# Perceiver block with routed experts: order of the first loads and products, and of the small vector work between routing and experts

## The chip, the cores and the metric

One core of a Trainium2 chip runs the whole program in one launch. The metric is device time in microseconds (us), the median of the runs. The engines run their own instruction streams and meet at semaphores: TensorE (PE), VectorE (DVE), ScalarE (ACT), GpSimd (POOL) and SyncE (SP), which here only issues DMAs.

## The reference, cut to what matters

```python
x = x + xattn(ctx, ctx, layernorm(x))     # 64 batches, 32 queries, 257 keys, width 256
x = x + linear_attention(layernorm(x))    # 16 heads of 64, causal sums over 32 tokens, gate
x = x + experts(layernorm(x))             # 8 experts, hidden 1024, top 2 by softmax

# xattn
qp = q @ Wq.T + bq; kp = k @ Wk.T; vp = v @ Wv.T + bv
probs = softmax(qp @ kp.T / sqrt(256))
out = (probs @ vp) @ Wo.T + bo

# experts
scores = xt @ gate_w.T
top_vals, top_idx = top_k(scores, 2); top_w = softmax(top_vals)
h = silu(xt @ w1.T) * (xt @ w3.T)         # per expert
y = sum over the two picked experts of top_w * (h @ w2.T)
```

All data is float32. There are 2,048 tokens.

## The kernel before

Tokens are handled as NT = 16 tiles of 128 rows (four batches each). Every engine has its own list of steps, written out by hand; a semaphore for each product says how many tiles have it.

**Folded weights.** The cross-attention does not form keys and values. At the start PE forms m_qk from wq and wk (L544), c_qk from wk and bq (L549), the out-weight w_vo from wv and WoT (L556), and the bias from bv, WoT and bo (L561, L562). For the last, DVE spreads bv over 128 columns into bvb (L1259). ACT copies each result from PSUM (L954 to L960) and counts s_ev; PE waits for s_ev 6 before the first step, and POOL waits for the bias too. Before that PE waits for the loads l_wqk (wq, wk, bq), l_wx (wv, WoT, bv, bo) and l_con (the table of constants con, which also holds the identity for transposes).

**Cross-attention steps.** xstep(t) on PE: scores(t) L594, the transpose tr(t+2) of the normed rows L572, pv(t-1) L613 and L616, qk(t+1) L582, filler matmuls L642, the transposes of the probabilities p_tr(t) L604 and L605, c_tr(t-1) L626, proj(t-2) L635. FILL says how many filler matmuls a step gets; each filler appears as two instructions in the trace. On ACT a step is xT_ev(t+2), exp(t), qk_ev(t+1), pT_ev(t), cT_ev(t-1). On DVE it is maxes(t), last_row(t) (which makes p_last), norm(t-1), x1(t-2), ln(t+3), and in the first steps the statistics of the rows by quarter(q): quarter 0 ahead of all, quarter 1 in step -2, quarters 2 and 3 in step -1. In step 0 DVE also takes variance(0, FIRST_LN[1]) and ACT its square root; the table of functions on ACT is changed for this and back for exp.

**Loads.** SP issues the loads in this order: Wq, Wk, bq, rows quarter 0 (512 KB), con (395 KB), Wv, WoT, bv, bo (weights 256 KB each), ctxT(0) (1028 KB), row quarters 1 to 3; then in load(t) for each step a piece of the next stage's weights (256 KB, every second step), ctxT(t) (two buffers, freed by scores(t-2)), ctxN(t) (three buffers) and a small ctxL(t).

**From routing to experts.** After the linear attention (L536 to L538 products) come logits, and DVE picks the top two of the last four tiles in top_two(2) (max, then max_index for each tile). It adds up the counts (r_both), PE forms ranks (L817 to L819) and raises r_rank, and places() reads them. Filler matmuls (warm, L813, two instructions each) stand around ranks. DVE then marks the place of each picked token within a tile (in_slot) and the tile (in_tile); PE sums the row numbers into slots (L870) and raises r_rows. DVE writes slot_row (r_done), which the gather on POOL needs, and tile_e, the expert of each of the 39 slot tiles (r_map), which ACT waits for before its first w_hi. Of the two softmax weights, w_h is the float16 value and w_l what is left of it, scaled; weight_rows(h) multiplies both with in_tile into what_w, PE sums them (L877, r_tab), DVE forms slot_w.

**Experts.** Each float32 product is three products of rounded parts: high and low of the weights (w_hi by ACT L1139, w_lo by DVE L1570) and of the rows (xh by ACT, xl by DVE L1663). up(t) on PE takes four chunks of the weights of slot tile t (six matmuls each, L536 to L538) and waits for one low part at a time; it follows xtr(t) L888, the transpose of the gathered rows, and ahead of the first stands warm(5). DVE makes low parts 0 and 1 of the first tile with up_lo(0, range(2), expert(0)), then x_lo(0), then parts 2 and 3. expert(t) reads the expert's number from tile_e into a register.

## Time and profile before

| | us |
|---|---|
| median of 3 runs | 843.13 |
| lowest, highest | 838.98, 844.96 |
| profiled execution, its own time | 840.18 |
| its span, first to last instruction | 838.3 |
| PE busy | 798.5 (95%) |
| DVE busy | 640.2 (76%) |
| ACT busy | 565.7 (67%) |
| POOL busy | 282.0 (34%) |
| share of the chain that ended last | PE 88%, DVE 4%, issue 2% |
| mean granted PE clock | 0.982 |

The chain is followed back from the last instruction to what released each step. "issue" is time in which an engine waited for nothing that the profile shows. PE's busy time is modelled for pipelined matmuls. In rows of instructions the bracket gives the idle time of the engine before it and what ended it.

### The profile page before, as it was taken

The numbers are of one execution on the slowest core, as the hardware profiler recorded it, in microseconds if no ns is written. First come the engines' busy times: TensorE is split into PE (matmuls) and PEld (weight loads), VectorE is DVE, ScalarE is ACT, GpSimd is POOL, SyncE is SP. The second block draws the span as 40 slices with busy tenths as digits, with TensorE's granted clock in tenths as the row PEclk, the third lists the DMA queues.
The fourth block names the chain that finished last, engine by engine and source line by source line (L and its number), as shares of the span: only waits on it lengthen the run. The fifth ranks groups of instructions, "written<-read, shape, count | busy, mean of one in ns | idle before, by whom it ended". The sixth has DMA issues, their size and how long they took to land.

```text
span 838.3 us, 24109 instructions
## 1 busy us (share of the span) xinstructions
PE 798.5 (95%) x9278; PEld 696.6 (83%) x9278; DVE 640.2 (76%) x1033; ACT 565.7 (67%) x879; POOL 282.0 (34%) x190
## 2 busy tenths in 40 slices
PE   6999999999999999997897999999999999999993
PEld 5566588998999999996886888998889888898883
DVE  4445543756757575674788999999999999999992
ACT  2645456554656665472256899999899999988971
POOL 1333384020220202010001345555555555555541
PEclk9999999999999999999699999999999999999997
DMA  9999920000000000004962445544555445554452
GB/s 339 415 417 415 384 80 2 2 16 16 15 28 3 28 3 28 18 13 183 426 260 70 120 132 149 148 133 125 140 154 137 132 126 144 156 136 128 127 144 42
DMA packets 31771, 115.92 MB, mean 138 GB/s; under 512 B 4465, under 2 KB 11570, under 8 KB 26578
## 3 DMA queue, kind: packets, MB, share of 16 engines
q1 hardware_dynamic: 22834, 100.17, 33.4%
q0 software_dynamic: 8864, 14.69, 8.2%
q8 instruction: 57, 0.93, 0.4%
q14 instruction: 16, 0.13, 0.0%
HBM read 105.27 MB, written 9.57 MB: 137 GB/s over the span
## 4 chain that ended last, share of the span: by engine, by line
PE 88%; DVE 4%; issue 2%; ACT 1%; DMA 1%; SPq 0%; POOL 0%; POOLq 0%; DVEq 0%; ACTq 0%
PE ps L536 23%; PE ps L538 22%; PE ps L537 22%; PE ps L925 4%; PE ps L741 3%; PE ps L712 2%; PE ps L582 2%; PE ps L635 2%; PE ps L594 2%; PE ps L616 1%; PE ps L888 1%; PE ps L613 1%; PE ps L572 1%; PE ps L807 1%; DMA bor<-in_bo 1%
## 5 line engine op out<-in xcount | busy, mean ns | idle before, releaser
L1570 DVE TENSOR_TENSOR w_lo<-w,w_hi 128x1024 fp32r<-128x1024 f32 x156 | 187.4, 1224 | 1.1 <-issue 1.1
L522 POOL DMA_INDIRECT out_x<-y_sb,slot_row x39 | 123.7, 3173 | 117.9 <-ACT y_sb L1171 117.9
L1139 ACT ACTIVATE w_hi<-w 128x1024 fp32r x156 | 161.2, 1060 | 2.4 <-DVE tile_e L1614 2.4
L536 PE MATMUL ps<-w_hi,xh 128*128 128x512 f32 x312 | 125.8, 403 | 1.4 <-DVE xl L1663 1.3
L538 PE MATMUL ps<-w_hi,xl 128*128 128x512 f32 x312 | 122.0, 391 | 0.0
L537 PE MATMUL ps<-w_lo,xh 128*128 128x512 f32 x312 | 121.6, 390 | 0.0
L536 PE MATMUL ps<-xT_hi,wa_hi 128*128 128x256 f32 x384 | 109.4, 285 | 2.1 <-issue 1.0
L537 PE MATMUL ps<-xT_lo,wa_hi 128*128 128x256 f32 x384 | 107.9, 281 | 0.0
L538 PE MATMUL ps<-xT_hi,wa_lo 128*128 128x256 f32 x384 | 107.8, 281 | 0.0
L1150 ACT ACTIVATE w_hi<-w_sb 128x1024 fp32r<-128x1024 f32 x78 | 82.6, 1063 | 27.7 <-DMA w_sb<-in_w 15.2
L510 POOL DMA_INDIRECT xs_sb<-xn_d,slot_row x39 | 67.3, 1726 | 98.8 <-PE ps L888 78.4
L536 PE MATMUL ps<-w_hi,hh 128*128 128x256 f32 x312 | 91.9, 295 | 2.9 <-DVE hl L1670 2.9
L1649 DVE TENSOR_TENSOR w_lo<-w_sb,w_hi 128x1024 fp32r<-128x1024 f32 x78 | 92.1, 1225 | 2.1 <-ACT w_hi L1150 2.1
L538 PE MATMUL ps<-w_hi,hl 128*128 128x256 f32 x312 | 88.9, 285 | 0.0
L537 PE MATMUL ps<-w_lo,hh 128*128 128x256 f32 x312 | 88.7, 284 | 0.0
L536 PEld LDWEIGHTS ps<-xT_hi,wa_hi 128*128 128x128 f32 x384 | 72.3, 188 | 3.4 <-issue 2.4
L537 PEld LDWEIGHTS ps<-xT_lo,wa_hi 128*128 128x128 f32 x384 | 72.4, 188 | 0.4
L538 PEld LDWEIGHTS ps<-xT_hi,wa_lo 128*128 128x128 f32 x384 | 72.3, 188 | 0.0
L1029 ACT ACTIVATE neg<-ps 128x512 f32<-128x512 f32 x64 | 38.3, 598 | 47.5 <-PE ps L538 47.5
L536 PEld LDWEIGHTS ps<-w_hi,xh 128*128 128x128 f32 x312 | 58.5, 188 | 13.5 <-DVE xl L1663 2.0
L538 PEld LDWEIGHTS ps<-w_hi,xl 128*128 128x128 f32 x312 | 58.5, 188 | 12.8
L537 PEld LDWEIGHTS ps<-w_lo,xh 128*128 128x128 f32 x312 | 58.6, 188 | 11.1
(219 smaller groups left out, 1767.3 us busy)
## 6 DMA issues: line engine op xcount, KB each, us to landing
w_sb<-in_w SPq DMA_DIRECT2D x78, 512.0 KB, 4.5
ctx_t<-in_ctxT SPq DMA_DIRECT2D x16, 1028.0 KB, 9.0
ctx_n<-in_ctxN SPq DMA_DIRECT2D x16, 1024.0 KB
w<-in_w SPq DMA_DIRECT2D x8, 2048.0 KB, 14.8
stage<-in_w_a SPq DMA_DIRECT2D x16, 256.0 KB, 8.7
x_all<-in_x SPq DMA_DIRECT2D x4, 512.0 KB, 9.3
out_x<-x_all POOLq DMA_DIRECT2D x8, 256.0 KB, 3.2
xn_d<-xn_first POOLq DMA_DIRECT2D x6, 256.0 KB, 2.8
```

The lines of the kernel that those rows point to most:

```text
L510: pool.indirect_dma_start(xs_sb[:, :], None, xn_d, bass.IndirectOffsetOnAxis(slot_row[:, t:t + 1], 0)).then_inc(f_xs, 16)
L522: pool.indirect_dma_start(out, bass.IndirectOffsetOnAxis(slot_row[:, t:t + 1], 0), y_sb[:, :], None, compute_op=ALU.add).then_inc(f_st, 16)
L536: pe.matmul(dst, l_hi, r_hi, start=first, stop=False)
L537: pe.matmul(dst, l_hi, r_lo, start=False, stop=False)
L538: return pe.matmul(dst, l_lo, r_hi, start=False, stop=last)
L741: m = pe.matmul(ps[h * HD:(h + 1) * HD, 4 + b, (s * FC + c) * T:(s * FC + c + 1) * T], v_sb[rows, s, (2 * c + h) * HD:(2 * c + h + 1) * HD ...
L925: m = pe.transpose(ps[:, 4 + c // 4, (c % 4) * P:(c % 4 + 1) * P], h_sb[:, c * P:(c + 1) * P], ident)
L1029: act.activation(neg[:, n % 2, :], ps[:, n % 4, :], ACT.Relu, scale=-1.0).then_inc(a_neg, 1)
L1139: act.activation(w_hi[:, c, :].rearrange("p (c n) -> p c n", c=DC), w13[:, bass.ds(e, 1), c % 2, :, c // 2 * 512:(c // 2 + 1) * 512].rearr ...
L1150: act.activation(w_hi[:, 4 + c, :], src, ACT.Copy).then_inc(f_dhi, 1)
L1570: dve.tensor_tensor(w_lo[:, c, :].rearrange("p (c n) -> p c n", c=DC), w13[:, bass.ds(e, 1), c % 2, :, c // 2 * 512:(c // 2 + 1) * 512].re ...
L1649: dve.tensor_tensor(w_lo[:, 4 + c, :], src, w_hi[:, 4 + c, :].bitcast(F32), ALU.subtract).then_inc(f_dlo, 1)
```

## The change

Four edits:

1. SP loads row quarter 0 first; Wq and Wk follow; bq gets its own semaphore l_bq and goes behind con; ctxT(0) goes ahead of Wv, WoT, bv and bo.
2. On PE the products for c_qk move into step -2 (key_bias), behind tr(0). Those for w_vo and the bias move into step 0 (out_weight, out_bias), between qk(1) and p_tr(0), in banks 6 and 7; c_tr(0) and proj(0) get waits for their evictions. ACT's evictions move likewise: c_qk in step -2, w_vo and bias behind qk_ev(1) in step 0. DVE makes bvb in step -1, ahead of quarters 2 and 3. Filler matmuls stay in step -1 only (before: one in -2, two in -1, two in 0, one in 1).
3. On DVE the difference of the two top logits (dv) is taken inside top_two(2), between max and max_index. The steps from e1p to w_h move from behind slot_row to ahead of places(). tile_e moves behind slot_row.
4. The expert's number e0 is read once, ahead of the wait for r_tab, and only low part 0 is made ahead of x_lo(0); parts 1 to 3 follow it.

```diff
@@ -302,7 +302,7 @@
-    l_con, l_wqk, l_wx, l_wo, l_z = (sem(n) for n in ("l_con", "l_wqk", "l_wx", "l_wo", "l_z"))
+    l_con, l_wqk, l_bq, l_wx, l_wo, l_z = (sem(n) for n in ("l_con", "l_wqk", "l_bq", "l_wx", "l_wo", "l_z"))
     XQ = 4
@@ -357,16 +357,16 @@
+        load_x(0)
         weight(wq, "Wq", l_wqk)
         weight(wk, "Wk", l_wqk)
-        sp.dma_start(bqc[:, :], a["bq"]).then_inc(l_wqk, 16)
-        load_x(0)
         sp.dma_start(con[:, :], a["con"]).then_inc(l_con, 16)
+        sp.dma_start(bqc[:, :], a["bq"]).then_inc(l_bq, 16)
+        load_ctxT(0, 0)
         weight(wv, "Wv", l_wx)
...
             sp.dma_start(buf[:, :], a[name]).then_inc(l_wx, 16)
-        load_ctxT(0, 0)
         for q in range(1, XQ):
@@ -538,29 +538,36 @@
-        pe.wait_ge(l_wqk, 16 * 3)
+        pe.wait_ge(l_wqk, 16 * 2)
         for dc in range(DC):
...
         m.then_inc(s_mm, 1)
-        for dc in range(DC):
+        pe.wait_ge(l_con, 16)
+
+        def key_bias():
+            pe.wait_ge(l_bq, 16)
+            for dc in range(DC):
+                for ec in range(DC):
+                    m = pe.matmul(ps[:, 1, dc:dc + 1], wk[:, ec, dc * P:(dc + 1) * P], bqc[:, ec:ec + 1],
+                                  start=ec == 0, stop=ec == DC - 1)
+            m.then_inc(s_mm, 1)
+            pe.wait_ge(s_ev, 2)
+
+        def out_weight():
+            pe.wait_ge(l_wx, 16 * 4)
+            for dc in range(DC):
+                for ec in range(DC):
+                    m = pe.matmul(ps[:, 6, dc * D:(dc + 1) * D], wv[:, ec, dc * P:(dc + 1) * P], wo[:, ec, :],
+                                  start=ec == 0, stop=ec == DC - 1)
+            m.then_inc(s_mm, 1)
+
+        def out_bias():
+            pe.wait_ge(s_bvb, DC)
             for ec in range(DC):
-                m = pe.matmul(ps[:, 1, dc:dc + 1], wk[:, ec, dc * P:(dc + 1) * P], bqc[:, ec:ec + 1],
-                              start=ec == 0, stop=ec == DC - 1)
-        m.then_inc(s_mm, 1)
-        pe.wait_ge(l_wx, 16 * 4)
-        pe.wait_ge(l_con, 16)
-        for dc in range(DC):
-            for ec in range(DC):
-                m = pe.matmul(ps[:, 2, dc * D:(dc + 1) * D], wv[:, ec, dc * P:(dc + 1) * P], wo[:, ec, :],
-                              start=ec == 0, stop=ec == DC - 1)
-        m.then_inc(s_mm, 1)
-        pe.wait_ge(s_bvb, DC)
-        for ec in range(DC):
-            pe.matmul(ps[:, 3, 0:D], bvb[:, ec, :], wo[:, ec, :], start=ec == 0, stop=False)
-        pe.matmul(ps[:, 3, 0:D], ones[0:1, :], bor[0:1, :], start=False, stop=True).then_inc(s_mm, 1)
-        pe.wait_ge(s_ev, 6)
+                pe.matmul(ps[:, 7, 0:D], bvb[:, ec, :], wo[:, ec, :], start=ec == 0, stop=False)
+            pe.matmul(ps[:, 7, 0:D], ones[0:1, :], bor[0:1, :], start=False, stop=True).then_inc(s_mm, 1)
@@ -622,6 +629,8 @@
             wait(pe, x_cT, t)
+            if t == 0:
+                pe.wait_ge(s_ev, 3)
             for dc in range(DC):
@@ -631,11 +640,13 @@
             wait(pe, x_x1, t)
+            if t == 0:
+                pe.wait_ge(s_ev, 6)
             for dc in range(DC):
...
-        FILL = {-2: 1, -1: 2, 0: 2, 1: 1}
+        FILL = {-1: 2}
@@ -645,8 +656,13 @@
             pv(t - 1, 1 - p)
+            if t == -2:
+                key_bias()
             qk(t + 1, 1 - p)
             fill(t)
+            if t == 0:
+                out_weight()
+                out_bias()
             p_tr(t, p)
@@ -952,12 +968,16 @@
         act.activation(m_qk[:, :, :], ps[:, 0, :].rearrange("p (c d) -> p c d", c=DC), ACT.Copy).then_inc(s_ev, 1)
-        act.wait_ge(s_mm, 2)
-        act.activation(c_qk[:, :], ps[:, 1, 0:DC], ACT.Copy).then_inc(s_ev, 1)
-        act.wait_ge(s_mm, 3)
-        act.activation(w_vo[:, :, :], ps[:, 2, :].rearrange("p (c d) -> p c d", c=DC), ACT.Copy).then_inc(s_ev, 1)
-        act.wait_ge(s_mm, 4)
-        act.activation(bias[:, :], ps[:, 3, 0:D], ACT.Copy).then_inc(s_ev, 3)
+
+        def key_bias_ev():
+            act.wait_ge(s_mm, 2)
+            act.activation(c_qk[:, :], ps[:, 1, 0:DC], ACT.Copy).then_inc(s_ev, 1)
+
+        def out_ev():
+            act.wait_ge(s_mm, 3)
+            act.activation(w_vo[:, :, :], ps[:, 6, :].rearrange("p (c d) -> p c d", c=DC), ACT.Copy).then_inc(s_ev, 1)
+            act.wait_ge(s_mm, 4)
+            act.activation(bias[:, :], ps[:, 7, 0:D], ACT.Copy).then_inc(s_ev, 3)
@@ -1000,10 +1020,14 @@
             xT_ev(t + 2, p)
+            if t == -2:
+                key_bias_ev()
             exp(t, p)
...
             qk_ev(t + 1, 1 - p)
+            if t == 0:
+                out_ev()
             pT_ev(t, p)
@@ -1254,9 +1278,11 @@
         dve.wait_ge(l_con, 16)
-        dve.wait_ge(l_wx, 16 * 4)
-        for ec in range(DC):
-            dve.tensor_scalar(bvb[:, ec, :], ones, bvc[:, ec:ec + 1], None, ALU.mult).then_inc(s_bvb, 1)
+
+        def value_bias():
+            dve.wait_ge(l_wx, 16 * 4)
+            for ec in range(DC):
+                dve.tensor_scalar(bvb[:, ec, :], ones, bvc[:, ec:ec + 1], None, ALU.mult).then_inc(s_bvb, 1)
@@ -1322,6 +1348,7 @@
             if isinstance(t, int) and t == -1:
+                value_bias()
                 quarter(2)
@@ -1476,6 +1503,8 @@
             wait(dve, g_max, ts.stop)
+            if ts.stop == NT:
+                dve.tensor_tensor(dv[:, :], m8[:, :, 1], m8[:, :, 0], ALU.subtract).then_inc(r_d, 1)
             for t in range(ts.start, ts.stop):
@@ -1579,7 +1608,12 @@
         dve.tensor_tensor(scan[0][:, 7 + NT, :], scan[0][:, 6 + NT, :], both[:, NT - 1, :], ALU.add).then_inc(r_both, 1)
-        dve.tensor_tensor(dv[:, :], m8[:, :, 1], m8[:, :, 0], ALU.subtract).then_inc(r_d, 1)
+        dve.wait_ge(r_e1, 1)
+        link(dve.tensor_scalar(e1p[:, :], e1[:, :], 1.0, None, ALU.add))
+        link(dve.reciprocal(top_w[:, :, 0], e1p[:, :]))
+        link(dve.tensor_tensor(top_w[:, :, 1], e1[:, :], top_w[:, :, 0], ALU.mult))
+        flat = top_w[:, :, :].rearrange("p t k -> p (t k)")
+        link(dve.tensor_copy(w_h[:, :], flat))
         places()
@@ -1608,36 +1642,32 @@
         in_slots(range(ACT_Q, TOP * NT // 4))
-        link(dve.tensor_tensor(cmp2[:, :, :], con[:, C_TILE:C_TILE + SLOT_TILES].rearrange("p (t a) -> p t a", a=1).to_broadcast([P, SLOT_TILES, E]),
-                               end[:, 4:].rearrange("p (a e) -> p a e", a=1).to_broadcast([P, SLOT_TILES, E]), ALU.is_ge))
-        link(dve.reduce_sum(tef[:, :], cmp2[:, :, :], AX.X))
-        dve.tensor_scalar(tile_e[:, :], tef[:, :], float(E - 1), None, ALU.min).then_inc(r_map, 1)
         def weight_rows(h):
...
+        link(dve.tensor_tensor(cmp2[:, :, :], con[:, C_TILE:C_TILE + SLOT_TILES].rearrange("p (t a) -> p t a", a=1).to_broadcast([P, SLOT_TILES, E]),
+                               end[:, 4:].rearrange("p (a e) -> p a e", a=1).to_broadcast([P, SLOT_TILES, E]), ALU.is_ge))
+        link(dve.reduce_sum(tef[:, :], cmp2[:, :, :], AX.X))
         dve.wait_ge(r_rows, 1)
...
         dve.scalar_tensor_tensor(slot_row[:, :], ps[:, 6, 0:SLOT_TILES], -1.0, spare[:, :], ALU.add, ALU.add).then_inc(r_done, 1)
-        dve.wait_ge(r_e1, 1)
-        link(dve.tensor_scalar(e1p[:, :], e1[:, :], 1.0, None, ALU.add))
-        link(dve.reciprocal(top_w[:, :, 0], e1p[:, :]))
-        link(dve.tensor_tensor(top_w[:, :, 1], e1[:, :], top_w[:, :, 0], ALU.mult))
-        flat = top_w[:, :, :].rearrange("p t k -> p (t k)")
-        link(dve.tensor_copy(w_h[:, :], flat))
+        dve.tensor_scalar(tile_e[:, :], tef[:, :], float(E - 1), None, ALU.min).then_inc(r_map, 1)
         link(dve.tensor_tensor(w_d[:, :], flat, w_h[:, :], ALU.subtract))
...
         weight_rows(1)
+        dve.wait_ge(r_map, 1)
+        e0 = expert(0)
         dve.wait_ge(r_tab, 1)
...
         dve.wait_ge(r_done, 1)
-        up_lo(0, range(2), expert(0))
+        up_lo(0, range(1), e0)
@@ -1682,7 +1712,7 @@
         x_lo(0)
-        up_lo(0, range(2, 4), expert(0))
+        up_lo(0, range(1, 4), e0)
         for t in range(2):
```

## Rows read from the trace of the kernel before

**Rows 1.** Chain of the first 60 us: start us, us, what
```profile
18.42 1.02 PE ps L594 x16
...
20.25 1.28 ACT L983
...
45.37 1.08 PE ps L594 x16
```

**Rows 2.** Busy us by stage: PE, PEld, DVE, ACT, POOL; PEclk, DMA share, GB/s
```profile
21.00:23.00 2.00, 0.87 (x6) 0.42 (x4) 0.86 (x4) 1.61 (x5) 1.92 (x3) 1.00 1.00 414
...
35.00:46.00 11.00, 10.97 (x110) 6.86 (x106) 4.79 (x17) 4.65 (x16) 3.29 (x4) 1.00 1.02 415
```

**Rows 3.** DMA view, 0 to 10 us, 40 slices of 0.25 us
```profile
GB/s 0 0 0 0 0 0 0 98 90 213 381 356 225 303 426 419 294 214 98 131 230 295 246 295 307 341 301 379 290 366 305 349 353 328 398 334 423 448 403 345
```

**Rows 4.** Timeline of SP: issue of ctxT(5), start us, us
```profile
35.35 0.33 SPq L358 DMA_DIRECT2D ctx_t<-in_ctxT  x1
```

**Rows 5.** DMA view of 35.3 to 35.5 us: size, us to landing
```profile
ctx_t<-in_ctxT SPq DMA_DIRECT2D x1, 1028.0 KB, 10.0
```

**Rows 6.** Timeline, 0 to 24 us: start us, us, engine line, out<-in [idle before]
```profile
5.58 3.78 PE L544 MATMUL ps<-wk,wq 128*128 128x256 f32 x8 [5.58 <-DMA bqc<-in_bq]
...
11.23 1.99 PE L556 MATMUL ps<-wo,wv 128*128 128x256 f32 x8 [0.88 <-DMA bor<-in_bo]
...
11.61 0.48 DVE L1259 TENSOR_SCALAR bvb<-con,bvc 128x128 f32<-128x128 f32 x2
...
13.06 1.03 PE L561 MATMUL ps<-wo,bvb 128*128 128x256 f32 x4
...
14.92 1.40 DVE L1214 BATCH_NORM_STATS2 bn<-x_all 128x6 f32<-128x256 f32 x4 [2.18 <-DMA x_all<-in_x]
...
16.76 2.70 DVE L1214 BATCH_NORM_STATS2 bn<-x_all 128x6 f32<-128x256 f32 x8
...
22.70 0.44 PE L604 MATMUL ps<-con,prob 128*128 128x128 f32 x2 [1.13 <-DVE p_last L1290]
...
23.18 0.59 PEld L594 LDWEIGHTS ps<-ctx_t,qkT 128*32 128x32 f32 x16 [0.22 <-DMA ctx_t<-in_ctxT]
```

**Rows 7.** Timeline, 431 to 453 us, columns as in rows 6
```profile
431.06 0.61 DVE L1494 TENSOR_TENSOR prod<-chosen,ps 128x128 f32<-128x128 f32 x2 [0.83 <-PE ps L819]
...
442.50 0.17 DVE L1625 TENSOR_SCALAR e1p<-e 128x16 f32<-128x16 f32 x1
...
443.13 3.90 ACT L1139 ACTIVATE w_hi<-w 128x1024 fp32r x4 [2.43 <-DVE tile_e L1614]
...
443.41 0.19 DVE L1630 TENSOR_TENSOR w_d<-top_w,w_h 128x32 f32<-128x32 f32 x1
...
443.86 0.83 DVE L1618 TENSOR_TENSOR what_w<-in_tile,w_h 128x640 f16<-128x640 f32 x1
...
446.95 1.25 PE L877 MATMUL ps<-what_w,in_slot 128*128 128x80 f16 x16 [0.72 <-DVE what_w L1619]
...
448.45 3.08 PE L813 MATMUL ps<-con 128*128 128x256 f32 x10
...
449.73 2.36 DVE L1570 TENSOR_TENSOR w_lo<-w,w_hi 128x1024 fp32r<-128x1024 f32 x2 [1.06 <-issue]
452.01 0.42 DVE L1663 TENSOR_TENSOR xl<-ps,xh 128x256 fp32r<-128x256 f32 x1
...
452.48 0.50 PE L536 MATMUL ps<-w_hi,xh 128*128 128x512 f32 x1 [0.94 <-DVE xl L1663]
```

**Rows 8.** DMA view of 443.2 to 444 us: first gather, us to landing
```profile
xs_sb<-xn_d,slot_row POOLq DMA_INDIRECT x1, 2.9
```

**Rows 9.** Busy time by stage, columns as in rows 2
```profile
402.00:404.00 2.00, 0.74 (x5) 0.65 (x5) 1.97 (x6) 0.38 (x1) 0.00 (x0) 0.55 1.03 426
...
447.00:448.00 1.00, 1.00 (x17) 1.00 (x17) 0.00 (x0) 0.02 (x1) 0.00 (x0) 0.50 0.00 0
...
490.00:510.00 20.00, 20.00 (x123) 17.71 (x122) 20.00 (x22) 18.20 (x24) 9.68 (x5) 1.00 0.47 131
```

## Prediction

> **What bounds the kernel now.** I read the views from the whole to the part: the page's shares and chain (the table above), then the chain of the first 60 us [rows 1], the busy table by stage [rows 2], the DMA queue and its landings [rows 3 to 5], and last the instructions in order of time in the two stretches that the change touches [rows 6, 7]. TensorE (PE) carries 88% of the chain. The change touches no stage in which PE works through long products; it touches the start (0 to 30 us) and the passage between routing and experts (430 to 453 us), where the chain leaves PE.
>
> In the cross-attention after the start there are two bounds side by side. PE is busy 10.97 of 11 us, and the DMA engines are busy all the time at 415 GB/s [rows 2]. One step takes half of 11.06 us and needs one ctxT (1028 KB), one ctxN (1024 KB) and half a piece of 256 KB: 2.24 MB, which at 415 GB/s takes 5.4 us. PE's step is 5.5 us, so the DMA wins only about 0.1 us a step. At the start it has no lead at all: the scores of step 1 wait for ctxT(1) at 23.18 [rows 6], and ctxT(5), issued at 35.35 [rows 4], lands 10.0 us later [rows 5], at 45.35, just when its scores begin (45.37 in the chain) [rows 1]. The reader should see here that no earlier start of PE brings step 1 or step 5 forward, unless the bytes come earlier.
>
> Between routing and experts VectorE (DVE) is the bound: it makes the weight rows from 443.86, PE sums them at 446.95, DVE then reads an expert's number (1.06 us "issue"), makes two low parts, and only then xl, for which the first expert product waits until 452.48 [rows 7].
>
> **The start.** What each part does, in time of before's trace:
>
> - The products of wq and wk (L544, 3.78 us) begin at 5.58 [rows 6]. Now the 512 KB of the first rows go ahead of the two weights and bq behind; at the 300 to 350 GB/s of that stretch [rows 3] this is about +1.5 us less bq's wait: begin 6.5, end 10.3. The first rows land before these weights, but their normalisation still waits for con, whose bytes stand behind the same ones as before (about 9.3).
> - Out of PE's queue ahead of the first step go the out-weight products (1.99 us, L556), their bias products (1.03 us for four, and two more of that width, 0.5) and the wait for bo at 11.23 [rows 6]. With transposes, key bias (under the 1.99 us of L556, since it is as many but narrower matmuls), qk(0) and two filler matmuls between, I get scores(0) at 14.7 instead of 18.42 [rows 1]: 3.7 us earlier.
> - That gain meets DVE. Before maxes(0) it must take the statistics of x quarters 1 to 3, and quarter 1 lands at 14.92. The bytes ahead of it are the same set in another order, so this doesn't move by the reordering. From there: 1.40 us, one xn, and from 16.76 on 2.70 us for two quarters, to 19.46 [rows 6]. Now bvb (0.48 us for two) stands in this queue as well, so maxes(0) would start 0.4 later than in before. What is won instead: ACT loads its exp table (1.28 us at 20.25 [rows 1]) while it waits, and not behind the maxes. So exp(0) begins near 20.5 instead of 21.54, 1.0 earlier. Its p_last, on which p_tr(0) (22.70) waited, comes 1.0 earlier too [rows 6].
> - The moved products now sit on PE between qk(1), which ends at about 18.2 (xn(2) at 16.65 leads), and p_tr(0): 3.5 us, to 21.7, about when p_last is there. Their two evictions (1.0 us) stand on ACT ahead of pT(0). They eat some of the 1.0. I get p_tr(0) at 21.7, tr(3) 0.4 us earlier than before.
> - scores(1) then waits for ctxT(1), whose time is set by bytes. The filler of step 1 (two matmul instructions, 0.5 us by the eight of L556) falls away, but behind it p_tr(1) needs p_last: I take 0.2 us. Together PE would be some 0.4 us ahead at step 2 and is caught by the DMA again by step 5.
>
> What can still come is an earlier DMA stream. Before, the moved rate falls to 98 and 131 GB/s between 4.5 and 5.0 us [rows 3], behind bq's small packets with the x load not yet begun. With 512 KB as the first transfer the queue doesn't run dry: at 320 GB/s lost for some 0.5 us at two thirds, and some at the neighbours, 0.4 us. The bounds are 0 (bq's and bv's small packets only move within the stream) and 0.9 (the dip and its neighbours gone). **Term 1: -0.4 us (0 to -0.9)**, carried by PE to the end of the stage and on.
>
> A page and a row differ on the stream. The row shows 415 GB/s from HBM to SBUF over 11 us [rows 2]. The Trainium skill, DMA: Bandwidth & Descriptors, section Where 436 GB/s comes from, says that for such transfers the HBM side binds at about 358 GB/s. By that figure a step would last 6.2 us and PE would wait in every one; the trace does not agree, and I keep the row.
>
> **Routing.** dv moves between max and max_index, into the chain of part 2: about +0.1 (an estimate, half of the 0.18 of its neighbours' form [rows 7], since small independent ones overlap). The four small instructions from e1p (442.50) to w_h, before w_d at 443.41, take 0.91 us and go into the wait for the ranks [rows 7]. That wait is 0.83 us, and dv's place in it falls free (0.1): next to nothing is left over. Should this cover be gone, they cost up to 0.9 there and the gain below is nil. **Term 2: +0.1.**
>
> **Weight rows.** w_d starts 0.91 earlier, less the reordering of tile_e behind slot_row, which leaves the sum of DVE's work the same: what_w starts at 443.0 instead of 443.86, and PE's last half of them (1.25 us at 446.95) begins at 446.1 [rows 7]. tile_e comes 0.4 us later, and with it ACT's four w_hi (443.13, 3.90 us): they end at 447.4, and the next that needs ACT is xh, after the transpose on PE near 447.8. So it is hidden; xh would be late only from a delay of about 0.8. Behind tile_e's wait nothing else of ACT stands. The gather of the first rows goes out behind slot_row, which is done when e1p starts at 442.50 and now comes 0.1 earlier; a us later on GpSimd's side and 2.9 us from issue to landing [rows 8] make some 446.4, ahead of need.
>
> **Low parts.** The expert's number is read before the wait for r_tab, under PE's 1.25 us: of the 1.06 us "issue" ahead of w_lo [rows 7] some 0.9 go. So w_lo(0) starts at 448.0 instead of 449.73 and ends at 449.2, and xl (0.42) follows it instead of the second one (1.2 less): 449.65, against 452.43 in before, 2.8 earlier. The other three low parts follow at 1.2 us each (2.36 for two [rows 7]), so the second is ready 1.2 us after the first product can begin.
>
> But PE has ten filler matmuls in its queue ahead of the first expert product: 3.08 us at the halved clock [rows 7, 9]. They follow the transpose, 0.85 earlier than now, and end at about 450.65. In before they had 0.94 us to spare; now they are what ends last. The first product starts at 450.65 instead of 452.48. From there DVE and PE are both full (20.00 of 20.00 us each from 490 on [rows 9]), and the first times and low parts of tile 1 depend on these products by the same distances, so the shift stays. **Term 3: -1.85**, bounds 0 (something not seen takes the place of xl) and -2.8 (full clock, no filler in the way).
>
> **Sum:** -0.4 + 0.1 - 1.85 = -2.15 us. The profiled execution took 840.18 us (838.3 span and 1.9 around it) and would take 838.0. It lies 2.95 under the median of the three runs (843.13); I put the change on the median: 841.0.
>
> **Rivals.**
> 1. *The clock stays up in the passage.* It is halved at 447 [rows 9], where PE had waited 1.84 and 0.72 us for weight rows [rows 7]; now the first wait is 0.9 shorter. Without the fall L877 takes 0.75, the filler 2.4: first product at 449.7, and the end at -3.0: 840.1. For it: shorter waits. Against: a second wait and its place remain.
> 2. *The intended gain arrives whole.* scores(0) is 3.7 earlier and all follows: -3.7 + 0.1 - 1.85 = -5.45, 837.7. Against it stand quarter 1 at 14.92 and ctxT(1) at 23.18 [rows 6].
> 3. *The passage brings nothing:* the small work spills over its 0.83 us and the filler, or ACT's later w_hi, holds xl: only term 1 and 2, and at most half of term 3: -1.2, 841.9 (to 842.8 for none).
> 4. *Slower.* Filler is taken from the first steps and PE has gaps before 17 and after 22 us. From 402 to 404 PE was busy 0.74 of 2 us and the clock went to 0.55 [rows 9]. If it falls so at 17 to 23, the 3.5 us of moved products take 7, p_tr(0) comes at 25.2 instead of 22.70, the DMA is then ahead and hides nothing: +2.5 there, term 1 hidden, +0.1 and -1.85: +0.75, 843.9. It decides once the products end after 22.7. Against: from 21 to 23 PE was busy 0.87 of 2 us and the clock stayed 1.00 [rows 2]. The Trainium skill, TensorE: Matmul & The Clock Gate, section HAM oscillation, says that long enough idle gaps on PE halve its clock; by that rule filler is not to be taken away, and the two rows disagree on whether gaps of this size do it.
>
> **Chances.** Forecast 0.45; rival 1 0.18, rival 2 0.07, rival 3 0.17, rival 4 0.13. The centres of 1, 3 and 4 lie within 840.1 and 843.9. The three runs before spread by 6 us around their median, which is more than the change, so I add some 3 us below and 1 us above: 836.5 to 845.0. A measurement of this kernel can tell about 1% (8.4 us) from no change; none of the cases reaches that. Faster by over 1%: 0.04 (rival 2 with a low draw), slower by over 1%: 0.03, within 1%: 0.93.
>
> **What would show it.** In the profile after: scores(0) near 14.7; 8 statistics ending near 19.5 with maxes right behind; exp(0) within 0.1 us of nmx and no table load between; out-weight products ending before p_last; a wait for ctxT at step 1 and near step 5, at 22.7 and 45.0; first what_w near 443.0 less the shift of the start; w_lo(0) within 0.4 us of slot_w; the first expert product right behind the filler and 1.9 us (beside the start's shift) earlier. I am wrong if ctxT(5) lands over 1 us earlier or later than 45.0, if clock in the first 25 us shows under 1.00, if xl is still what the first product waits for, or if some wait among tiles 1 to 5 of the experts gives the 1.85 us back.

## The result and the profile after

| | before | after |
|---|---|---|
| median, us | 844.05 (12 runs) | 836.00 (12 runs) |
| lowest, highest | 838.98, 846.63 | 831.99, 837.58 |
| profiled execution, its own time | 840.18 | 833.98 |
| its span | 838.3 | 832.1 |
| PE busy | 798.5 | 796.2 |
| mean granted PE clock | 0.982 | 0.981 |

The ratio is 0.9909, 95% interval [0.989, 0.9928]: 7.7 us faster. That is just inside the 1% that the prediction called its limit of what can be told, but outside its range (836.5 to 845.0) by 0.5 us, and more than three times its 2.15 us. The sign was right. The forecast was put on a median of before of 843.13 from three runs; over twelve it is 844.05.

The first view of the kernel after is the timeline of the start (start us, us, engine line, out<-in, in brackets the idle time before). The rows answer [rows 6].

```profile
7.02 3.78 PE L544 MATMUL ps<-wk,wq 128*128 128x256 f32 x8 [7.02 <-DMA wk<-in_Wk]
...
14.70 1.08 PE L601 MATMUL ps<-ctx_t,qkT 128*32 128x257 f32 x16
...
16.88 1.89 PE L562 MATMUL ps<-wo,wv 128*128 128x256 f32 x8
...
20.19 0.44 PE L611 MATMUL ps<-con,prob 128*128 128x128 f32 x2
...
21.93 1.07 PE L601 MATMUL ps<-ctx_t,qkT 128*32 128x257 f32 x16 [1.20 <-DMA ctx_t<-in_ctxT]
```

The same stretch on DVE and ACT:

```profile
13.69 1.41 DVE L1238 BATCH_NORM_STATS2 bn<-x_all 128x6 f32<-128x256 f32 x4 [4.55 <-DMA x_all<-in_x]
...
15.71 2.71 DVE L1238 BATCH_NORM_STATS2 bn<-x_all 128x6 f32<-128x256 f32 x8
18.34 0.41 DVE L1307 TENSOR_REDUCE mx<-ps 128x1 f32<-128x257 f32 x1
...
16.58 1.28 ACT L1003 ACT_TABLE_LOAD   x1
18.97 0.48 ACT L1003 ACTIVATE prob<-ps,nmx 128x257 f32<-128x257 f32 x1 [1.10 <-DVE nmx L1309]
```

Scores(0) run at 14.70, quarter 1 lands at 13.69, the table load lies in ACT's wait, and PE then waits for ctxT(1) until 21.93.

The passage from routing to experts, which answers [rows 7]:

```profile
428.55 0.61 DVE L1523 TENSOR_TENSOR prod<-chosen,ps 128x128 f32<-128x128 f32 x2 [1.67 <-PE ps L835]
...
440.43 0.82 DVE L1648 TENSOR_TENSOR what_w<-in_tile,w_h 128x640 f16<-128x640 f32 x1
...
442.05 0.75 PE L893 MATMUL ps<-what_w,in_slot 128*128 128x80 f16 x16 [0.92 <-DVE what_w L1649]
...
443.52 0.75 PE L893 MATMUL ps<-what_w,in_slot 128*128 128x80 f16 x16 [0.72 <-DVE what_w L1649]
...
444.35 2.32 PE L829 MATMUL ps<-con 128*128 128x256 f32 x10
...
444.88 1.23 DVE L1599 TENSOR_TENSOR w_lo<-w,w_hi 128x1024 fp32r<-128x1024 f32 x1
...
446.03 0.42 DVE L1693 TENSOR_TENSOR xl<-ps,xh 128x256 fp32r<-128x256 f32 x1
...
446.50 0.50 PE L536 MATMUL ps<-w_hi,xh 128*128 128x512 f32 x1
```

From prod (the picks multiplied with their ranks) to the first expert product it takes 17.95 us; before it took 21.42 (431.06 to 452.48 in [rows 7]). The weight sums take 0.75 us, not 1.25, and the filler 2.32, not 3.08.

A third part of the gain lies where nothing was changed. In the linear attention DVE starts each tile with an instruction att<-att,den. Laid over each other by it, the profiled executions differ by -1.1 us at 150 and -1.0 at 264, by -0.5 at 295, -1.7 at 332 and -4.57 at 398 to 402. The timeline of PE shows what went. Of before:

```profile
319.63 0.39 PE L536 MATMUL ps<-xT_hi,wa_hi 128*128 128x256 f32 x1 [1.03 <-issue]
...
379.45 1.28 PE L712 MATMUL ps<-qT,kT 64*32 64x32 f32 x128 [0.25 <-issue]
383.19 0.39 PE L536 MATMUL ps<-wa_hi,xT_hi 128*128 128x512 f32 x1 [2.46 <-issue]
```

And of after at the same place of the program:

```profile
377.56 1.33 PE L728 MATMUL ps<-qT,kT 64*32 64x32 f32 x128
378.82 0.50 PE L536 MATMUL ps<-wa_hi,xT_hi 128*128 128x512 f32 x1
```

Before, PE stood 2.46 us behind 128 short products and 1.03 us at 319.63, each time for nothing that the profile shows ("issue"; I call such an idle time a stall). After, neither is there. Others are: 0.69 us at 281.57, where before has none over 0.3, and 1.83 at 402.31, where before has 0.76 at 405.77. From 60 to 440 us the stalls of over 0.3 us add up to 6.30 us before and 4.12 after.

The whole pair: start -1.1, the two stalls and their surroundings -3.5, last tile to the end of top_two +0.5 (the longer stall at 402.31 lies here), ranks +1.5 (they stand behind filler at the low clock: prod came 3.92 us after the picks, before 2.38), passage -3.5, experts -0.2. The sum, from unrounded terms, is -6.2.

### The profile page after: what moved, and what is told of

The parts are those of the page before. It is cut to its first block, busy times and chain, and to the rows that moved or that the text cites. A ratio compares the mean times of both kernels' runs of the same rounds, so it can differ in the third digit from the quotient of the medians.

```text
span 832.1 us, 24093 instructions
## 1 busy us (share of the span) xinstructions
PE 796.2 (96%) x9270; PEld 695.7 (84%) x9270; DVE 637.9 (77%) x1033; ACT 564.5 (68%) x879; POOL 281.5 (34%) x190
## 4 chain that ended last, share of the span: by engine, by line
PE 89%; DVE 4%; DMA 3%; issue 2%; ACT 1%; POOL 0%; POOLq 0%; SPq 0%; DVEq 0%; ACTq 0%
PE ps L536 23%; PE ps L538 22%; PE ps L537 22%; PE ps L941 4%; PE ps L757 3%; PE ps L728 2%; PE ps L589 2%; PE ps L646 2%; PE ps L601 2%; PE ps L623 1%; DMA ctx_t<-in_ctxT 1%; PE ps L904 1%; PE ps L620 1%; PE ps L829 1%; PE ps L823 1%
## 6 DMA issues: line engine op xcount, KB each, us to landing
w<-in_w SPq DMA_DIRECT2D x8, 2048.0 KB, 14.3
```

## The experiments

The kernels of the table ran 6 to 12 times each, and before 23 to 33 times beside them on the same chip; the ratios are to those runs. Each run has one profiled execution, to which all places and stalls below belong. All compute the whole reference.

| run | median, us | ratio to before [95%] |
|---|---|---|
| start_only | 838.18 | 0.9932 [0.9912, 0.9952] |
| passage_only | 840.18 | 0.9951 [0.9928, 0.9975] |
| fill_only | 841.32 | 0.9975 [0.9951, 0.9999] |
| small_only | 842.22 | 0.9978 [0.9947, 1.0008] |
| lo_only | 842.12 | 0.9986 [0.9959, 1.0013] |
| products_only | 846.01 | 1.0039 [1.0006, 1.0072] |
| loads_only | 847.25 | 1.0032 [1.0005, 1.006] |
| after_pad4 | 837.93 | 0.9949 [0.9921, 0.9976] |
| after_pad4_late | 838.61 | 0.9946 [0.9917, 0.9975] |
| after_warm1 | 836.54 | 0.9911 [0.9871, 0.9951] |
| after_nofill | 834.46 | 0.9902 [0.9874, 0.993] |

One execution each: before_again 844.34, after_pad2_late 833.36, after_pad8_late 842.29, after_pad16_late 857.47.

### Start and passage apart

**start_only**: edits 1 and 2. **passage_only**: edits 3 and 4. The diffs are the parts of the change above.

```diff
 start_only:   edits 1, 2 as in the change; passage as before
 passage_only: edits 3, 4 as in the change; start as before
```

> Edits 1 and 2 alone (loads, first products, filler). Theory A: the loads bring the stream of bytes about 1.1 us earlier, and PE's idle stretches named issue at 319.6 (1.03), 383.2 (2.46) and 389.6 us (1.36) go or shrink because PE's instruction stream is shorter ahead of them and its fetched blocks begin elsewhere: about -4.5 us in all, and the same places and sizes of issue stretches before 400 us as in the changed kernel. Rival B: these stretches fall anew in every execution, whatever the code: -1.1 us in the median, and other stretches than in the changed kernel.

> Edits 3 and 4 alone. PE's stream ahead of the routing is as before. Theory A: the issue stretch of 2.46 us before 383.2 stays; the passage from the ranks to the first expert product is 2 to 3.5 us shorter; time -2.5 to -3.5 us. Rival B: the same time, but the stretch of 2.46 us is likely gone or elsewhere.

Measured: -5.7 us and -4.1 us by the ratios (intervals 4.1 to 7.4 and 2.1 to 6.1). The passage took 20.91 us in start_only and 17.93 in passage_only. start_only has the stalls of the changed kernel (0.98 at 385.83), passage_only those of before (1.28 at 322.48, 2.17 at 385.73), as theory A had it in both. So the start's edits brought at least as much as the passage, where the prediction gave them 0.4. The two together make -9.8, more than the 7.7 of the whole change; their intervals are wide enough for this.

**before_again**, unchanged:

> The kernel before, profiled once more. Theory A: the same issue stretches on PE before 400 us at the same distance from the start, 0.69, 1.03, 2.46 and 1.36 us within 0.3. Rival B: other places or sizes.

Stalls of 1.13 us at 320.29 and 2.17 at 383.45 were there again: they belong to the kernel, not to one execution. The passage took 21.15; in fill_only, loads_only and products_only, where it is unchanged too, 21.40 or 21.41.

### Filler or stream length

```diff
-        FILL = {-2: 1, -1: 2, 0: 2, 1: 1}
+        FILL = {-1: 2}
```

> Only the filler matmuls of steps -2, 0 and 1 are taken out (four fewer, eight instructions in the trace), nothing else. The start itself can win 0.2 us at most. Theory A: the issue stretches before 400 us lie and measure otherwise than before and the time changes by 1 to 3.5 us. Rival B: no change of the time (within 0.5 us).

It gained 2.1 us (interval 0.1 to 4.1). The start of its profiled execution was one of the slowest (scores(0) at 20.92), but its PE timeline has no stall at 320 or 383. With four fewer filler matmuls, PE's stream is 16 instructions of the trace shorter there.

To tell the filler from the length, **after_pad4** restores the length by four products that nothing reads:

```diff
             proj(t - 2, p)
+            if t == 0:
+                for _ in range(4):
+                    pe.matmul(ps[:, 1, 0:1], ident, con[:, 0:1], start=True, stop=True)
```

> The changed kernel with four matmuls of one column added on PE ahead of the scores of step 1, where PE waits 1.2 us for ctxT(1). They have no use and lengthen PE's stream by the same number of instructions (16 in the trace) that the taken filler had. Theory A (the stalls hang on where PE's stream falls into its blocks): the issue stretches of before come back near 320 (1.1 us) and 383 (2.2 us), and the time is 3 us longer than the changed kernel's (some 839 against 836). Rival B: the stretches stay as in the changed kernel and the time with them (836).

The start was as in the changed kernel (scores(1) at 22.33, the first att<-att,den at 149.94 against 149.64), and both stalls came back. PE of after_pad4:

```profile
319.11 0.28 PE L538 MATMUL ps<-xT_hi,wa_lo 128*128 128x256 f32 x1 [0.86 <-issue]
...
382.39 0.50 PE L536 MATMUL ps<-wa_hi,xT_hi 128*128 128x512 f32 x1 [2.17 <-issue]
```

The median rose by 1.9 us, against the 3 expected; the intervals of the two ratios overlap a little (up to 0.9928 and from 0.9921), so this difference alone is not certain. **after_pad4_late** puts the same four into step 12, far from the start:

```diff
-            if t == 0:
+            if t == 12:
```

> The changed kernel with the same four one-column products as in the run after_pad4, but put in step 12 (near 90 us) instead of step 0, so that nothing of the start is touched. Theory A (the stalls of PE near 319 and 382 depend on how many instructions stand in PE's stream ahead of them): the stalls come back (0.8 us or more near 320, 2 us or more near 383), the first att<-att,den still stands near 149.8, and the median is 837.5 to 839, 1.5 to 3 us above the changed kernel. Theory B (the stalls follow from something in the first steps, such as the start's timing or its loads): no stall above 0.5 us there and the time of the changed kernel, 836.

```profile
321.04 0.28 PE L538 MATMUL ps<-xT_hi,wa_lo 128*128 128x256 f32 x1 [0.84 <-issue]
...
384.77 0.80 PE L536 MATMUL ps<-wa_hi,xT_hi 128*128 128x512 f32 x1 [2.71 <-issue]
```

Theory A held: both are back, and the median is 2.6 us over the changed kernel's, of which the padding itself takes about 0.9 in step 12, where it is not hidden by a DMA (the first att<-att,den came at 151.20, not at the 149.8 expected).

Then three lengths more, one execution each: two, eight and sixteen of the padding products in step 12.

```diff
-                for _ in range(4):
+                for _ in range(2):      # 8, 16
```

> The changed kernel with two of the one-column products in step 12 (eight more trace instructions, half way between the changed kernel's stream and that of before). Theory A (a stall shows only where the end of a block of PE's instructions falls on a stretch of short ones, so each placement has its own set): sum of the issue stalls from 190 to 400 us between the 2.8 us of the changed kernel and the 6 us of before, with one of the two near 320 and 383 there. Theory B (the stalls of 320 and 383 are there or not by chance from execution to execution): no relation to the length; either both or none.

> The same with eight products (32 more trace instructions, 16 beyond the length of before). Theory A: the stalls near 320 and 383 are there as in before, or have moved by a few instructions; those near 198 and 283 may be gone or longer. Theory B: they are absent as often as present.

> The same with sixteen products (64 more trace instructions). Theory A: the set of stalls changes again; if blocks are short against 64 instructions it returns to one of the sets already seen, if they are long the stalls of 320 and 383 move to other lines of the same stage. Theory B: no relation.

PE of after_pad2_late, then of after_pad8_late:

```profile
380.92 0.50 PE L537 MATMUL ps<-wa_lo,xT_hi 128*128 128x512 f32 x1 [1.07 <-issue]
...
386.23 0.29 PE L731 MATMUL ps<-qT,kT 64*32 64x32 f32 x15 [1.05 <-issue]
```

```profile
320.64 0.26 PE L731 MATMUL ps<-qT,kT 64*32 64x32 f32 x5 [0.78 <-issue]
380.15 0.24 PE L760 MATMUL ps<-att,v_sb 32*64 32x32 f32 x2 [1.02 <-issue]
385.42 0.27 PE L731 MATMUL ps<-qT,kT 64*32 64x32 f32 x8 [2.21 <-issue]
```

The sum of PE's stalls of over 0.3 us, by the number of PE's matmuls in the page:

| matmuls | kernels | 315 to 395 us | 60 to 440 us |
|---|---|---|---|
| 9266 | after_nofill | 1.83 | 4.35 |
| 9270 | after, start_only, fill_only, and after_warm1 (5 fillers fewer, all behind this stretch) | 0.97 to 1.25 | 4.12 to 4.67 |
| 9274 | after_pad2_late | 2.46 | 4.17 |
| 9278 | before, before_again, small_only, lo_only, passage_only, products_only, loads_only, after_pad4, after_pad4_late | 3.46 to 4.85 | 5.77 to 8.07 |
| 9286 | after_pad8_late | 4.01 | 8.05 |
| 9302 | after_pad16_late | 3.29 | 13.31 |

Sixteen products moved them again: 1.34 us at 186.87, 1.32 at 369.43, 2.26 at 397.95, 4.55 at 427.45 are the longest. after_pad2_late has 3.1 us of stalls from 190 to 400, between the changed kernel's 2.3 and before's 5.5, as theory A had it. The nine executions of 9278 matmuls, from eight kernels, all have the two stalls at the same two places of the program, and the four of 9270 have neither. Theory B of these three runs, chance from execution to execution, is out. Over the whole stretch the nine have 6.63 us of stalls on the mean and the six shorter ones 4.27: 2.4 us less, close to what fill_only gained (2.1) and the two pads of four gave back (1.9 and 2.6).

The place is fixed more closely than by the length. Count PE's matmuls from the front (the x in PE's busy column, from 0 to just ahead of a stall). Of before, of after_pad4, then of before and of after:

```profile
0.00:383.18 383.18, 366.97 (x6276) 1.00 0.32 121
0.00:382.38 382.38, 366.03 (x6276) 1.00 0.32 122
0.00:405.76 405.76, 384.79 (x6654) 1.00 0.34 132
0.00:402.30 402.30, 383.51 (x6654) 0.99 0.35 134
```

In the 17 traces the stalls between 190 and 415 us stand behind 2464, 4242 or 4243, 5004 or 5005, 6276, 6403 or 6654 matmuls (not each one in every execution); with eight and sixteen products in step 12 there are further ones, each about a whole multiple of 127 matmuls away from one of these. So the stall stays at its place in the stream, and the program is shifted under it. On the DMA side, the queue for instructions moves blocks of 16,384 bytes. Its packets of the 2.46 us stall (before, 380.0 to 383.3 us):

```profile
q8 instruction: 1, 0.02, 2.4%
```

This packet ended at 381.82, 1.37 us ahead of the stall's end. The distance is 1.2 to 1.6 us for every stall of over 0.3 us from 60 to 440 us in the 17 traces, with one exception (1.72, at the 4.55 us stall). PE goes on a nearly fixed time after a block has come in. All this fits PE waiting for its own instructions; no run varied the blocks themselves.

The longest stall also has a consequence that the pair of before and after doesn't show. Eleven executions have the stall of 2.2 to 2.7 us behind 6276 matmuls; in eight of them (small_only, lo_only, passage_only, products_only, loads_only, after_pad4_late, after_pad8_late, after_pad16_late) the granted clock fell to its lower level within 1.2 us of the stall's end, for 3.4 to 10.2 us. In the six executions without it the clock did not fall there. From the matmul behind the stall to the 522nd after it, stalls left out, PE took 31.4 to 33.3 us where the clock fell and 29.3 to 30.7 where not. How often it falls in the executions that were not profiled is not known; before, before_again and after_pad4 had the stall without the fall.

after_pad16_late also shows something else. It was 24 us slower than after_pad2_late, 12.6 of them by the first att<-att,den. Its busy table by stage (PE, PEld, DVE, ACT, POOL, PEclk, DMA share, GB/s):

```profile
32.00:35.00 3.00, 1.45 (x19) 0.53 (x17) 1.43 (x3) 0.56 (x3) 2.87 (x4) 1.00 1.01 412
35.00:37.00 2.00, 2.00 (x16) 0.89 (x16) 0.87 (x4) 0.88 (x3) 0.00 (x0) 0.69 1.03 427
37.00:40.00 3.00, 3.00 (x20) 2.02 (x13) 0.48 (x1) 0.00 (x0) 0.00 (x0) 0.50 1.01 410
```

PE had waited 1.55 us for a ctxT (scores(2) at 34.06), then the clock fell to its lower level and the next step took 8.74 us (scores at 34.06 and 42.80) instead of 5.53, before any padding had run. Step 12 with its padding followed (3.8 us for the sixteen), and scores(13) at 97.62 took 1.94 us, at half speed again. The fall near 35 is the mechanism of rival 4, in one of nine executions with the new start, behind a DMA wait.

### The start taken apart

**products_only** moves only the products (edit 2 without the new FILL), **loads_only** only the loads (edit 1).

```diff
 products_only:
-        load_x(0)
         weight(wq, "Wq", l_wqk)
         weight(wk, "Wk", l_wqk)
+        sp.dma_start(bqc[:, :], a["bq"]).then_inc(l_bq, 16)
+        load_x(0)
         sp.dma_start(con[:, :], a["con"]).then_inc(l_con, 16)
...
-        FILL = {-1: 2}
+        FILL = {-2: 1, -1: 2, 0: 2, 1: 1}
```

(against the changed kernel's start; ctxT(0) behind bo again.)

> Of the start, only the new place of the products of edit 2 (key bias, out weight, bias, and DVE's bvb), with the old order of loads and the old filler; PE's stream is as long as before. Theory A (the moved products bring the start's gain, as they stand where PE waits anyway and their slow executions are hidden): first att<-att,den near 150, scores(0) at 16 to 17, ratio 0.995 to 0.998; the stalls near 320 and 383 are there, as the stream has its old length. Theory B (the loads bring it): att<-att,den between 150 and 155 as in before and ratio 0.998 to 1.001.

> Before with only the new order of the first loads and bq's own semaphore; all products, filler and the passage as before. Theory A (loads bring nothing by themselves, since the out-weight products still stand ahead of the first scores): ratio 0.999 to 1.002, the out-weight products later than in before (WoT lands behind ctxT(0)), scores(0) 19 to 22, and scores(1) 24 or later. Theory B (the earlier DMA stream carries the gain): scores(1) at 22.3 or earlier, ratio 0.994 to 0.997.

Both are slower than before, by 3.3 and 2.7 us (intervals 0.5 to 6.1 and 0.4 to 5.1). Theory A of products_only missed (first att<-att,den at 153.21); of loads_only, theory A named the right places (scores(1) at 24.29) but a ratio of at most 1.002. PE of products_only:

```profile
17.83 1.08 PE L601 MATMUL ps<-ctx_t,qkT 128*32 128x257 f32 x16
...
20.88 1.89 PE L562 MATMUL ps<-wo,wv 128*128 128x256 f32 x8
...
24.18 0.44 PE L611 MATMUL ps<-con,prob 128*128 128x128 f32 x2
```

The scores start only at 17.83, so the moved products end at 24.18, where before p_tr(0) stood at 22.70 [rows 6]. In loads_only the out-weight products wait for bo behind ctxT(0), until 12.55, and the scores come at 19.68:

```profile
12.55 1.99 PE L557 MATMUL ps<-wo,wv 128*128 128x256 f32 x8 [0.97 <-DMA bor<-in_bo]
...
19.68 1.08 PE L595 MATMUL ps<-ctx_t,qkT 128*32 128x257 f32 x16
```

Together, and with four fewer fillers, they gain 5.7 us (start_only), of which the stalls are some 2: the products have to be gone from ahead of the scores, and the scores' data have to be early. Both together with the old fillers were not run.

What the start brought can be read from the first att<-att,den. With the old start it stood at 150.74 (before), 149.97, 152.66, 155.26 and 154.00 in five executions (mean 152.5), and at 154.45 in fill_only; with the new one at 149.64 (after), 150.04, 149.94, 149.78 and 149.62 (mean 149.8; after_nofill and the runs with four or more products in step 12 left aside). The profiled execution of before was one of its good ones: the gain is 2.7 us on the mean and 1.1 in that pair. PE of small_only:

```profile
11.41 3.78 PE L556 MATMUL ps<-wo,wv 128*128 128x256 f32 x8 [1.06 <-DMA bor<-in_bo]
...
21.17 1.08 PE L594 MATMUL ps<-ctx_t,qkT 128*32 128x257 f32 x16
```

So in the four late executions PE, and not the bytes, was what scores(1) waited for: ctxT(1) had landed at 22.0 to 23.3 and the scores came at 24.4 to 25.8. With the new start the out-weight products stand where PE waits for ctxT(1) anyway, behind the rise, and took 1.89. In the two executions of that start with a late rise and the filler of step -1 (16.2 in start_only, 15.9 in after_pad2_late) scores(1) came at 22.76 and 22.30, and the first att<-att,den at 150.04 and 149.62, as in those with a rise at 11.2 to 12.4. The new start makes the kernel indifferent to when the clock rises, within that reach.

**after_nofill** takes the last filler out as well:

```diff
-        FILL = {-1: 2}
+        FILL = {}
```

> The changed kernel without the last filler of the first steps (eight more trace instructions less in PE's stream). Theory A (where the stream falls decides the stalls near 320 and 383, and a further shift can bring them back, move them or leave them out): the stalls stand at another place than in the changed kernel or are the same as in it; time within 2 us of the changed kernel, with the difference equal to the sum of the stalls. Theory B (filler in step -1 keeps the clock up): granted clock under 1.00 in the first 25 us and the first att<-att,den over 1 us later than 149.6, ratio to before 0.993 or more.

```profile
16.54 1.94 PE L601 MATMUL ps<-ctx_t,qkT 128*32 128x257 f32 x16 [0.81 <-ACT qkT L995]
```

Here scores(0) took 1.94 us instead of 1.08 and the first att<-att,den came at 152.04, 2.4 later than in the changed kernel. The first rise of the clock came at 19.6, later than in any other execution. That this is for want of the filler is not shown: up to 13.7 us both kernels run the same stream, and in six of the eight executions with the new start and the filler the clock had risen by 12.4, before the filler began. And the time is the changed kernel's (0.9902 against 0.9909, intervals overlapping), so theory B missed in the ratio, and theory A held, with the stalls behind the same counts of matmuls as elsewhere. The 2.4 shrink to 1.7 at the first expert product and 0.5 at the end; why is open.

### The passage taken apart

**small_only** is edit 3 alone, **lo_only** edit 4 alone.

```diff
 small_only:
-        dve.tensor_tensor(dv[:, :], m8[:, :, 1], m8[:, :, 0], ALU.subtract).then_inc(r_d, 1)
+        dve.wait_ge(r_e1, 1)
+        link(dve.tensor_scalar(e1p[:, :], e1[:, :], 1.0, None, ALU.add))
...
 lo_only:
+        dve.wait_ge(r_map, 1)
+        e0 = expert(0)
         dve.wait_ge(r_tab, 1)
...
-        up_lo(0, range(2), expert(0))
+        up_lo(0, range(1), e0)
```

> Of the change only edit 3 (dv, the steps e1p to w_h and tile_e moved). Theory: what_w starts 0.9 us earlier after the ranks, the waits of PE for it are shorter (0.92 instead of 1.84 us) and the clock stays at 1.00 until the first expert product: -0.9 and -0.5 for the second L877 group, up to the first product -1.4 us. Rival (the shorter wait has no bearing on the clock): it falls near 447 to 454 us as in the four profiles without the edit, -0.9 us.

> Of the change only edit 4 (the expert's number read ahead of r_tab, one low part ahead of xl). DVE could have xl 2.0 us earlier. Theory: the clock falls here as in before, and the filler of 3.08 us holds PE, so the first product comes only some 0.9 us earlier than before after the ranks and starts right behind the filler. Rival: the filler does not hold it, -2.0 us.

From prod to first expert product took 19.98 and 20.04 us, each 1.4 less than in before and the three others with 21.4; both together 17.93 to 17.95, 3.5 less. Neither alone is told from no change by its ratio. The missing 0.7 us is the filler at the low clock: in lo_only xl was ready at 456.14 and the first product began at 456.88. PE of lo_only, then of small_only:

```profile
451.24 0.75 PE L877 MATMUL ps<-what_w,in_slot 128*128 128x80 f16 x16 [1.83 <-DVE what_w L1619]
452.71 1.25 PE L877 MATMUL ps<-what_w,in_slot 128*128 128x80 f16 x16 [0.72 <-DVE what_w L1619]
...
456.88 0.58 PE L536 MATMUL ps<-w_hi,xh 128*128 128x512 f32 x1
```

```profile
452.68 0.75 PE L877 MATMUL ps<-what_w,in_slot 128*128 128x80 f16 x16 [0.72 <-DVE what_w L1622]
...
457.70 0.50 PE L536 MATMUL ps<-w_hi,xh 128*128 128x512 f32 x1 [1.88 <-DVE xl L1664]
```

In lo_only PE had waited 1.83 us, the clock fell, and although xl was early the first product stood behind the slow filler, at 456.88, just as the forecast had it for the whole change. With edit 3 the wait is 0.92 us and the clock stays at its upper level. Of the 17 executions, seven had the wait of 1.83 us (before, before_again, start_only, fill_only, lo_only, loads_only, products_only) and in all seven the clock fell behind it, in start_only only 1 us behind the first product. Nine had 0.91 or 0.92 us (all with edit 3 but after_warm1) and in none it fell, not even in small_only, where PE waited a further 1.88 us for xl. The edits and the wait go together here, so this says nothing of other places.

**after_warm1** takes filler away ahead of ranks, since the ranks stood behind it at the low clock:

```diff
-            warm(6)
+            warm(1)
```

> The changed kernel with one filler matmul instead of six ahead of the ranks. DVE has the counts ready while PE still has filler in its queue (5.3 us at the halved clock); without it the ranks follow the counts. If that queue is what costs: -1 to -1.5 us (834.7). Rival: with less filler the clock is low for longer and what follows takes more: 0 or up to +2 us.

prod came 3.07 us after the picks instead of 3.92, but the passage behind took 19.12 us instead of 17.95 (the low clock that had begun at 417.8 lasted to 434.9, where after's ended at 428.1), and the time is the changed kernel's. No gain, as the rival had it.

## Why the prediction was wrong, point by point

**The start, term 1 (-0.4; measured -1.1 in the pair, -2.7 on the mean).** Some of its events were right: scores(0) at 14.70 (forecast 14.7), the table load hidden, the wait for ctxT(1) (21.93, forecast 22.7). Two things were mis-sized. Quarter 1 landed at 13.69, not 14.92, and so maxes(0) began at 18.34 instead of near 19.9. Over the executions its mean was 14.3 with the old loads (seven) and 13.8 with the new ones (ten): of the 1.2 the order may explain about 0.5, the rest was chance. For ctxT(1) the means are 22.5 and 22.0, so the gain in bytes was sized about right, at 0.4. And PE was not caught by the DMA again at step 5: scores(1) to (3) began as their ctxT landed (21.89, 27.81, 33.31), but ctxT(5) landed at 43.98, 0.4 ahead of its scores at 44.41, with PE busy all the time. That is 1.0 us ahead of the 45.0 forecast, the prediction's own sign of being wrong.

The step that failed was taking one execution's start for the start: the products ahead of the scores took 1.99 us in the one that I had and 3.8 in most, because the clock rose at 9.7 us in that one and near 15 in most. That no earlier start of PE brings step 1 forward holds for that execution and not for the late ones, where the scores of step 1 came 1.7 to 3.7 us behind ctxT(1). To move the products under a wait takes away that risk, which no sum over one trace shows.

**The long middle (0; about -3.5 at 398 us in the pair, -2.5 with the longer stall at 402).** The prediction wrote that the change touches no stage of long products and carried the shift of the start unchanged to 430. That step failed. It counted the removed filler at its 0.5 us, and did not ask what a shorter stream does to all that follows. The stalls of 1.03 and 2.46 us were there to be read in before's trace; on the mean of the executions the shorter stream is worth 2.4 us of stalls.

**Routing, term 2 (+0.1).** The four small instructions did go under the wait for ranks. But this wait grew from 0.83 to 1.67 us in this pair, since the low clock lay under the filler there; over the executions it varies with where the low clock falls (picks to prod 2.38 and 4.39 in two executions of before). The least with edit 3 is 2.45 and without it 2.38, the 0.1 of the forecast; no run shows the 1.5 as a cost of the change.

**The passage, term 3 (-1.85; measured -3.5).** Each piece was right: what_w 0.92 earlier behind prod (forecast 0.86), w_lo(0) 0.58 after slot_w where it had been 1.50, one low part ahead of xl instead of two (1.13). The step that failed was the choice between the forecast and rival 1: I held the clock as halved and so the filler as the last to end. It stayed up, for the reason that rival 1 names (shorter waits), and xl stayed the last to end, by a hair: the first product began 0.06 us behind xl's end (0.05 in before), and the last filler matmul would have made way for it at the same time. Rival 1's -2.8 for this term (its three terms make -3.1, not the -3.0 written) is 0.7 short of the measured value: it took xl from the forecast, at 449.65, where the weight sums still had their slow 1.25 us. With 0.75 for them slot_w, w_lo and xl all come 0.5 earlier too; the other 0.2 is spread over pieces that each came a little earlier than forecast. The row for the clock, 443 to 444 and 446 to 447 us of after:

```profile
443.00:444.00 1.00, 0.48 (x14) 0.49 (x15) 0.46 (x1) 1.00 (x3) 0.00 (x0) 1.00 0.35 115
446.00:447.00 1.00, 1.00 (x6) 0.70 (x5) 1.00 (x3) 0.48 (x1) 0.00 (x0) 1.00 0.32 106
```

It is 1.00 where before had 0.50 [rows 9]. The Trainium skill, TensorE: Matmul & The Clock Gate, section HAM oscillation, was cited for the opposite worry, that idle gaps halve the clock. The trace agrees with it in the passage, where shortening a gap from 1.83 to 0.92 us kept the clock up.

**The experts.** As forecast: the shift is -5.98 us at the first product, -5.8 in tiles 1 to 3 and -6.1 to -6.25 from there to the end; nothing is given back.

**Rivals.** Rival 2's mechanism did not happen: the 3.7 us of scores(0) met quarter 1 and ctxT(1); that its 837.7 lies near the result is accident. Rival 3 fell with the passage. Rival 4 did not happen in the pair and did in one execution (after_pad16_late), at another place than I had put it. The sign that the prediction set for it, a granted clock under 1.00 in the first 25 us, cannot be read ahead of the first record (11.7 us in after).

**The range.** Its lower end took 3 us for the spread of runs and none for a cause outside the two stretches. Start on the mean (-2.7), the stalls (by their sums, by fill_only and by the two pads, -1.9 to -2.6) and the passage (-3.5) make -8.1 to -8.8, against -7.7 measured (interval -9.3 to -6.1). What the clock's falls behind the longest stall add to this is not known.

## What to carry to other kernels

A change of a few instructions early in a long unrolled stream can be worth more through where the rest of the stream falls than through what it removes: list the "issue" idle times of the bounding engine over the whole span first, and when a measured gain is larger than its cause, pad the stream back to its old length before naming a cause. Before comparing two starts, look at when the clock first rose in each. Work whose time varies from execution to execution belongs under a wait that is there anyway. Two edits that fail or give little alone (loads or products; less small work or an earlier low part) can be worth making together, where each removes the wait that would take the other's place.

## What the runs showed of the hardware

- **Idle time of PE without a wait.** Stalls of 0.3 to 2.7 us (one of 4.55), most of them behind or within the groups of 128 short products (L712, L741, 128 matmuls in 1.3 us), the others in the products right behind such a stage. They stand at fixed counts of matmuls from the front of the stream, about 127 or a multiple apart, and end 1.2 to 1.6 us (once 1.72) after a block of 16,384 bytes has come over the queue for instructions. That PE waits for such a block is inferred from the fixed place and the fixed distance; no run varied the block or its load.
- **The first rise of the clock.** It came 4.1 us after PE's first product in before and 12.7 us after it in products_only, and varies between executions (9.7 to 17.2 us where the loads or the products are the old ones, 11.2 to 19.6 where both are new). The eight products of L544, the first of all, took 3.77 or 3.78 us in all executions but one (3.38 in loads_only, where the rise came at 10.3, before they ended). What PE must do for the rise was not found.
- **Narrow products and the clock.** Of the pads with one column, each takes 0.23 us, so that eight take 1.84 of PE's time. Behind these eight PE was busy all the time and the clock still fell, at 93.1 us; behind sixteen it fell too, at 97.2, and behind the four of after_pad4_late it did not, in one execution each. Timeline and busy table of after_pad8_late:

```profile
89.19 1.84 PE L671 MATMUL ps<-con 128*128 128x1 f32 x16
```

```profile
92.00:96.00 4.00, 4.00 (x30) 2.31 (x27) 1.35 (x5) 0.87 (x3) 0.17 (x1) 0.64 0.96 370
```
